# Attention outputs in column strips of the array, two or four heads side by side, with the row sums as a second product

## What is computed

```python
# second block: 16 heads; self: 16 features each, causal; cross: 8 features each
p = jax.nn.softmax(scores.astype(jnp.float32), axis=-1).astype(q.dtype)
return jnp.einsum('bhqk,bhkd->bhqd', p, v)
# third block: 16 heads of 64 features, keys masked
attn = jax.nn.softmax(sim, axis=-1)
out = jnp.einsum('bhij,bhjd->bhid', attn, v)
```

## Time and profile before

| | us |
|---|---|
| median of 3 runs | 887.32 |
| lowest and highest | 886.87, 887.95 |
| span of the profiled execution | 888.7 |
| TensorE busy with matmuls | 815.3 (92%) |
| VectorE, ScalarE, GpSimd busy | 438.5, 419.3, 160.7 |

### The profile page before, as it was taken

How to read it: one execution, slowest core, us unless ns; L and a number is a source line. 1 busy time by engine, 2 the same in 40 slices (tenths; PEclk the granted TensorE clock), 3 DMA queues, 4 the chain that set the end, 5 groups by cost and what they waited for, 6 DMA issues and landing times.

```text
span 888.7 us, 13138 instructions
## 1 busy us (share of the span) xinstructions
PE 815.3 (92%) x4696; PEld 698.1 (79%) x4696; DVE 438.5 (49%) x898; ACT 419.3 (47%) x815; POOL 160.7 (18%) x240
## 2 busy tenths in 40 slices
PE   4799899999999999999876979999999999999996
PEld 3578778788887788889655868788888977888894
DVE  0645335364674766332435263363554936663314
ACT  3413344456452566554434333454573445666444
POOL 0204303040021333000003160042200303330000
PEclk9888899999999999999987978999999999999998
DMA  9200000003003000000180000000040120000001
GB/s 338 84 0 1 1 2 1 1 1 122 40 1 142 1 1 1 1 1 1 41 316 31 1 1 1 1 1 1 1 161 1 33 111 1 1 2 1 1 1 53
DMA packets 5835, 33.28 MB, mean 37 GB/s; under 512 B 1288, under 2 KB 2696, under 8 KB 4488
## 3 DMA queue, kind: packets, MB, share of 16 engines
q1 hardware_dynamic: 4904, 31.21, 9.3%
q10 hardware_dynamic: 864, 1.19, 0.4%
HBM read 31.36 MB, written 1.05 MB: 36 GB/s over the span
## 4 chain that ended last, share of the span: by engine, by line
PE 74%; DVE 13%; ACT 7%; issue 5%; DMA 1%; ACTq 0%; SPq 0%; DVEq 0%
PE ps_B L736 7%; PE ps_A L736 7%; PE ps_B L589 3%; DVE max_B L1510 2%; PE ps_A L710 2%; PE ps_A L589 2%; PE ps_A L671 2%; PE ps_B L806 2%; PE ps_A L806 2%; PE ps_A L602 2%; PE ps_B L671 2%; PE ps_B L710 2%; PE ps_B L877 2%; PE ps_A L877 2%; PE ps_A L854 2%
## 5 line engine op out<-in xcount | busy, mean ns | idle before, releaser
L736 PE MATMUL ps_A<-probs_A,v_A 128*128 128x256 f32 (+1 forms) x384 | 98.7, 381 | 2.9 <-ACT probs_A L1170 2.9
L736 PE MATMUL ps_B<-probs_B,v_B 128*128 128x256 f32 (+1 forms) x384 | 96.3, 375 | 5.2 <-ACT probs_B L1170 4.3
L736 PEld LDWEIGHTS ps_B<-probs_B,v_B 128*128 128x128 f32 x384 | 67.0, 193 | 14.5 <-ACT probs_B L1170 6.7
L736 PEld LDWEIGHTS ps_A<-probs_A,v_A 128*128 128x128 f32 x384 | 68.9, 199 | 10.5 <-ACT probs_A L1170 4.3
L710 PE MATMUL ps_B<-q_B,kz_B 128*128 128x256 f32 x192 | 62.4, 375 | 2.0 <-ACT q_B L1151 1.7
L710 PE MATMUL ps_A<-q_A,kz_A 128*128 128x256 f32 x192 | 62.1, 372 | 1.4 <-ACT q_A L1151 1.3
L1170 ACT ACTIVATE probs_A<-ps_A 128x384 f32<-128x384 f32 (+1 forms) x64 | 34.4, 545 | 56.7 <-PE ps_A L712 30.9
L473 POOL TENSOR_SCALAR kz_A<-big_A,const 128x256 fp32r<-128x256 f32 x32 | 29.9, 952 | 160.5 <-DVE big_A L1484 160.5
L671 PE MATMUL ps_A<-kz_A,q_A 128*128 128x256 f32 x192 | 51.9, 371 | 4.2 <-DVE max_A L1508 3.9
L463 POOL TENSOR_SCALAR kz_A<-big_A,const 128x256 fp32r<-128x256 f32 x64 | 38.3, 615 | 92.9 <-ACT big_A L1112 92.9
L671 PE MATMUL ps_B<-kz_B,q_B 128*128 128x256 f32 x192 | 51.5, 363 | 2.2 <-DVE q_B L1490 2.2
(11 more groups left out here) (344 smaller groups left out, 1965.2 us busy)
## 6 DMA issues: line engine op xcount, KB each, us to landing
ffn_w<-in_l1m SPq DMA_DIRECT2D x2, 3072.0 KB, 18.7
ffn_w<-in_l2f SPq DMA_DIRECT2D x2, 3072.0 KB, 11.1
attn_w<-in_l1a SPq DMA_DIRECT2D x2, 2432.0 KB, 11.7
attn_w<-in_l2q SPq DMA_DIRECT2D x2, 2048.0 KB, 8.4
gm_w<-in_gm SPq DMA_DIRECT2D x5, 640.0 KB, 3.9
v_B<-in_l1d SPq DMA_DIRECT2D x2, 1408.0 KB, 7.0
big_B<-in_trig SPq DMA_DIRECT2D x1, 832.0 KB, 7.3
v_A<-in_x SPq DMA_DIRECT2D x2, 256.0 KB, 6.1
```

Source lines behind the costliest of these rows:

```text
L736: last = mm(L.ps[:, 2 + g % 2, lo:S], L.values(a, h0 + h, kt), L.probs[:, at + lo:at + S], start=(h % GROUP[a] == 0 and kt == 0), stop=(h ...
```

## The change

Heads are taken in batches: `TILES = [4, 4, 2]` heads at once, each in its own strip of `TILE = [32, 32, 64]` array columns and the same PSUM partitions. `weigh` is called once for each batch, and issues two products for each head: first the values, then (`sums`) a stationary operand of ones from the constants, into the other half of the same bank. Each product has one matmul for each 128 keys; within a batch the strips follow one another in the innermost loop. Groups become `GROUP = [8, 16, 2]`, so a group fills all 128 rows with outputs and another 128 rows with sums. There are 11 groups per lane and pass instead of 22, and lines 1179, 1180 and 1529 now work on 128 rows.

A batch needs all its probabilities at once, with a second set for the next batch: they stand in `big`, `probs` and the upper half of `big2` (`weights`). The steps of an attention stage become `heads + 2`. With four strips `weigh` comes at steps 5, 9, 13 and 17, with two strips at steps 3, 5, 7 and 9, where it was at every step from 1 on. `PLAN` is not touched. Heads are scored in the order of `head_order`.

The tile `v` has a region for each attention, so GpSimd no longer resizes it between them, and its clearing covers 2048 columns instead of 4208.

```diff
-GROUP = [4, 8, 1]
+GROUP = [8, 16, 2]
+TILES = [4, 4, 2]
+TILE = [32, 32, 64]
...
+            def weights(self, a, i):
+                turn, j = i // TILES[a] % 2, i % TILES[a]
+                if a == LATENT:
+                    return self.big[:, (2 * turn + j) * 512:(2 * turn + j + 1) * 512]
+                if turn == 0:
+                    return self.big[:, j * 512:(j + 1) * 512]
+                if j < 2:
+                    return self.probs[:, j * 512:(j + 1) * 512]
+                return self.big2[:, j * 512:(j + 1) * 512]
...
+        def sums(a, h):
+            n = TILE[a] // HEAD_DIM[a]
+            at = [K_SUM16 + 16, K_SUM8 + 24, K_ONES][a] - (HEAD_DIM[a] * (h % n) if a < LATENT else 0)
+            return const[:, at:at + TILE[a]]
...
-                def resize_for_cross(L):
...
-                def resize_for_latent(L):
...
-                    def weigh(h):
-                        n = n0 + h
-                        g = (h0 + h) // GROUP[a]
...
-                        pe.wait_ge(*L.probs_ready.at(it, n + 1))
...
-                        for kt in range(ST):
-                            lo = kt * P if a == SELF else 0
-                            at = (h % 2) * 512 + (1 - kt) * S
-                            last = mm(L.ps[:, 2 + g % 2, lo:S], L.values(a, h0 + h, kt),
-                                      L.probs[:, at + lo:at + S],
+                    def weigh(b):
+                        g = order[b * tiles] // GROUP[a]
...
+                        pe.wait_ge(*L.probs_ready.at(it, n0 + (b + 1) * tiles))
...
+                        for part in range(2):
+                            for kt in range(ST):
+                                lo = kt * P if a == SELF else 0
+                                for j in range(tiles):
+                                    h = order[b * tiles + j]
+                                    at = (1 - kt) * S
+                                    out = L.ps[j * TILE[a]:(j + 1) * TILE[a], 2 + g % 2, part * S + lo:(part + 1) * S]
+                                    last = mm(out, sums(a, h) if part else L.values(a, h, kt),
+                                              L.weights(a, b * tiles + j)[:, at + lo:at + S],
...
-                    for h in range(heads + 1):
-                        if h < heads:
-                            scores(h)
-                        if h >= 1:
-                            weigh(h - 1)
+                    for step in range(heads + 2):
+                        if step < heads:
+                            scores(step)
+                        if step > tiles and (step - 1) % tiles == 0:
+                            weigh((step - 1) // tiles - 1)
...
-                        r = L.recip[0:64, (g % 2) * S:(g % 2 + 1) * S]
+                        r = L.chunk(L.recip, g % 2)
```

More of the change, by code:

```diff
@@ L51, with head_order @@
 SCALE = [16 ** -0.5, 8 ** -0.5, 64 ** -0.5]
-GROUP = [4, 8, 1]
 SHARE = [2, 4]
-V_PAD = 56
-VROW = V_PAD + HEADS * P
+GROUP = [8, 16, 2]
+TILES = [4, 4, 2]
+TILE = [32, 32, 64]
+V_AT = [0, ST * 512, 2 * ST * 512]
+V_ROW = [512, 512, INNER]
+V_END = V_AT[LATENT] + ST * INNER
+def head_order(a, h0, heads):
+    order = []
+    for g in range(h0, h0 + heads, GROUP[a]):
+        turns = GROUP[a] // TILES[a]
+        order += [g + turns * j + i for i in range(turns) for j in range(TILES[a])]
+    return order
 def columns(*sizes):
@@ L184, in build @@
         vec_step = signal("vec_step", 74)
-        act_step = signal("act_step", 58)
+        act_step = signal("act_step", 36)
         class Lane:
@@ L426, in _ @@
                     wait(*L.sq_ready.at(it, 1))
-                    nc.gpsimd.memset(L.v[:], 0.0).then_inc(L.v_cleared.sem, 1)
-                    wait(*L.v_cleared.at(it, 1))
-                    for kt in range(ST):
-                        last = nc.gpsimd.memset(L.slots(kt, 64, HEAD_DIM[SELF]), 1.0)
-                    last.then_inc(L.v_cleared.sem, 1)
-                def resize_for_cross(L):
[L434 to L438, removed]
-                def resize_for_latent(L):
[L442 to L449, removed]
+                    nc.gpsimd.memset(L.v[:, 0:V_AT[LATENT]], 0.0).then_inc(L.v_cleared.sem, 1)
                 def stacked_keys(L, a):
@@ L1169, in exps @@
                             lo = P if a == SELF else 0
[L1170 removed]
+                            last = fn(dst[:, lo:512], L.ps[:, i % 2, lo:512], ACT.Exp, scale=SCALE[a])
                         last.then_inc(L.probs_ready.sem, 1)
                     def reciprocals(g):
[L1175 to L1176 removed]
+                        r = L.chunk(L.recip, g % 2)
+                        act.wait_ge(*L.pv_done.at(it, BLOCK_BASE[block] + (g + 1) * GROUP[a] // tiles - h0 // tiles))
                         if g >= 2:
                             act.wait_ge(*L.head_out.at(it, GROUP_BASE[a] + g - 1))
[L1179 removed]
+                        step.done(fn(r, L.half(2 + g % 2, 1), ACT.Ln))
                         fn(r, r, ACT.Exp, scale=-1.0).then_inc(L.recip_ready.sem, 1)
[L1182 to L1186 removed]
+                    for i in range(heads + 2):
+                        if i < heads:
+                            exps(i)
+                        if i > 1 and (i - 1) % GROUP[a] == 0:
+                            reciprocals((h0 + i - 1) // GROUP[a] - 1)
                         yield
```

118 lines of the change are left out of this document (56 added, 62 removed).

## The result

The changed kernel takes 892.87 us (median of 7 runs, 889.29 to 895.35), the kernel before took 886.94 us in 7 runs beside it: a ratio of 1.0049, 95% interval 1.0027 to 1.0071. It is slower by half a per cent, some 4 to 6 us, where +41.7 us were predicted. One term must be wrong by at least about that much, or several by parts of it.

The account below looks back on a forecast made before the run. TensorE, busy 92% of the span, was taken as the bound: 887.3 + 0 (products) + 19.8 (width changes) + 21.8 (waits) = 929 us. Its own range was 915 to 940 us, the 8-in-10 range 876 to 1000 us.

Parts of the forecast that it names:

- The products: Attention products on TensorE after the change: every batch keeps its old time, 0 us, bounds -48 and +152 us.
- two at once: Product batches: only one strip's second pass and the next strip's first overlap, 0.216 us per matmul, 0 us; chance 0.41.
- the rival: All strips of a product batch stream at once: -48.4 us in self and cross, 883 us in all; chance 0.27.
- the 2.38x: The skill's three-strip speed-up, taken for every batch of four, would give something near the bound of -48 us.
- The changes of width: Switching strip width around each of 64 batches idles TensorE 0.31 us, +19.8 us in all, bounds 18.6 to 21.
- The waits: TensorE waiting for ScalarE and VectorE in self of B and both cross stages: +21.8 us, bounds half to 28.
- One of those gaps: Cross of lane A: VectorE, taking maxima, runs dry 1.3 us beneath a batch, adding +1.8 us.
- a bound of 4: Waits in the latent stages: taken as 0, though up to 0.5 us per stage, 8 x 0.5, was possible.

Follow-up runs that it names:

- after: The changed kernel itself, with heads batched in column strips, against the kernel before: 892.87 us, ratio 1.0049.
- run 3: Changed kernel with the loop over strips outermost, so a strip's whole work of a batch precedes the next strip's: 996.49 us, ratio 1.123 to the kernel before.
- run 5: Changed kernel with a product's loops swapped, two matmuls of one strip in a row, then the next strip's two: 894.9 us, ratio 1.0067 to the kernel before.
- Run 1: Changed kernel with latent products back at 128 columns, one head at a time, self and cross keeping strips: 880.48 us, ratio 0.992 to the kernel before.
- run 4: Kernel before with self and cross products in batches of four heads, one step later, at full array width without strips: 928.28 us, ratio 1.047.
- Run 2: Changed kernel without the products of row sums in self and cross, the logarithm reading a constant: 883.98 us, ratio 0.996 to the kernel before.

## Why the prediction was right and wrong

**The products: the step that failed.** I set them at 0 between -48 and +152 us, "two at once", because the second pass of a strip would hold back all strips behind it, and "in all rows the passes begin in the order of the program". Those rows had no two strips side by side, so they could not tell. After shows -48.4 us: a batch in 1.77 us. Runs 3 and 5 show the rule in its place: a strip holds four passes, the one that streams counted, and only a fifth holds back the rest; passes of different strips overtake each other. The innermost loop over strips, which I named in favour of the rival, was the evidence that decided; it gives each strip only two passes in a row.

The Trainium skill, "TensorE: Matmul & The Clock Gate", Part 3, says that matmuls start and end in strict program order. By run 3 that does not hold across strips of fp32 passes: a pass at 194.86 us starts ahead of one at 195.07 that comes first in the program. "TensorEngine Tiling (Array Packing)", Theoretical Speedup, in the Trainium skill gives up to 4x for 32 columns, and here the trace agrees: 0.055 against 0.216 us. My use of the 2.38x from Part 3 of the Trainium skill's page on TensorE was wrong as well: with twice the passes it leaves 2 / 2.38 = 0.84 of the 97 us, which makes an estimate of 15 us saved and not something near 48.

That the direction came out right is luck: with the products at -48.4 and the other terms as I had them, my own sum gives 880.5 us, faster than before.

**The changes of width: right.** 0.31 us predicted, 0.32 to 0.33 measured; 64 x 0.325 = 20.8 against 19.8 us. Run 1 took 32 of them back and won 12 us.

**The waits: right for the changed kernel, for a reason that was half right.** Per pass, predicted and measured growth of TensorE's idle time: self of A (with the piece behind it) 0 and -0.3, self of B 2.0 and 3.6, cross of A 4.4 and 4.3, cross of B 4.5 and 3.7. In all 10.9 and 11.2, for two passes 21.8 and 22.5 us. But those numbers were worked out for batches of unchanged length, and for these run 4 shows 13.9 per pass in idle time and 40.5 us in all. So the agreement is in part luck. What I missed is that the blocks themselves stand in the other lane's chain, all four of them: I priced only the gaps under them. One of those gaps can be held against its row: VectorE was to run dry for 1.3 us beneath a batch of cross of A; with the full-width batches of run 4 it does for 2.18, with the short ones for 0.79. Three latent stages of a pass are 1.8 to 2.0 us longer, where the changes of width account for 1.3, and the last one is as long as before: beyond the changes some 0.5 us per pass, 1 us in all, which I had set at 0 with a bound of 4.

**The clock: not in the sum.** The mean granted clock of the profiled executions fell from 0.962 to 0.952. With two levels, 1.0 and 0.5, that is 2 x (1 - 0.962) x 888.7 = 67.5 us at the lower one before and 85.8 after. If TensorE works through all of it, half of the 18 us more, 9 us, is lost. In the first pass the stages above hold 7 us of the 18: self of A has 0.82 for 0.89 and cross of B 0.92 for 1.00. Cross of B is slow in both passes of after; other places move from run to run.

**The sum again:** -48.4 + 20.8 + 22.5 + 1 + up to 9 = up to +5 us; measured are +6 between the medians and +5 between the two profiled executions. The rival with all strips at once (883 us) had the products right, and the waits within 2 us; what it lacked is the clock. The small loss is a balance of large terms: waits, width changes and clock cost what four strips gain and a little more.

**What stays open.** In experiment 4 the profiled executions differ by 34.9 us and not by the 40.5 of the medians. 33.4 us of them lie in these stages: 27.7 us of idle time in two passes, and 5.7 us that TensorE is busy longer; which row holds those I did not separate. What sets the clock back where is not settled either. Run 2 shows that it can fall where TensorE has less to do, and run 5 that the same wait can pass without a fall. No run holds the clock fixed, so its share of the 6 us, and what run 2 would have saved, stay estimates.

## What to carry to other kernels

Column strips pay by the number of strips less what is added: four strips with doubled work halve the stream, two strips with doubled work gain nothing and pay 0.32 us for each change of width. Use them where a batch streams for much longer than that, and keep the strip loop inside, so that no strip has more than four fp32 passes in a row. Before crediting a saving in a stage, ask whether TensorE or the other lane's chain ends it: with TensorE busy for 95% of the way through these stages before, it seemed the only bound, but with the batches in it the other lane's chain was as long, to 0.2 us, as the stage had been, and it took over at once. Batching makes blocks, and a block costs twice: once for what waits for it, once for what it no longer covers. After such a change, look at the small interrupting instructions again; a step of plan for one copy was worth as much as the whole net loss. And when stages of two traces are compared, count from the same event in both: the same time on the two axes is not the same point of the work.

## What the runs showed of the hardware

- The four strips of 32 columns take fp32 passes at 0.055 us each, all of them streaming at once; two strips of 64 at 0.11.
- A strip holds four passes, the one that streams counted (runs 3 and 5), and passes of different strips start out of program order (195.07 ahead of 194.86 in the program of run 3).
- A change between 128 and 32 columns costs 0.10 to 0.12 us on the way in and 0.20 us on the way out, with all operands ready.
- Less work for TensorE can go with a lower granted clock: 0.89 in cross of A without the sums, 1.00 with them, at the same stage length. The same idle time can do without: 1.62 of 3.00 us busy, then 0.57 in after and 1.00 in run 5.
